# A slot order of an attention and mixture-of-experts kernel: pairs of score maxima behind the scores, VectorE's other work ahead of the maxima, top-2 steps spread over two slots, routing weights multiplied by GpSimd

## The reference, cut to what matters

```python
h = _layernorm(x) * (1 + ca) + sa
q, k, v = (split_heads(binlinear(h, W, b)) for W, b in ((Wq, bq), (Wk, bk), (Wv, bv)))
att = softmax(einsum('bhtd,bhsd->bhts', q, k) * scale)
x = x + ga * binlinear(merge(einsum('bhts,bhsd->bhtd', att, v)), Wp, bp)
h = _layernorm(x) * (1 + cb) + sb
shared = einsum('bsi,hi->bsh', silu(h @ shared_gate.T) * (h @ shared_up.T), shared_down)
probs = sigmoid(h @ router_w.T + routing_bias)
scores, indices = top_k(probs, 2)
scores = scores / sum(scores)                       # the two routing weights of a token
combined = sum over the two chosen experts of score * (silu(h @ gate_w[e]) * (h @ up_w[e])) @ down_w[e]
x = x + gb * (shared + combined)
```

## Time and profile before

| | |
|---|---|
| three runs | 663.35, 664.64, 675.9 us; median 664.64 us |
| profiled execution | 667.65 us, span 665.6 us |
| mean granted TensorE clock of its span | 0.969 of full speed |
| attention's paired slots | 78.03 to 464.14 us of the span |
| busy share of the span: TensorE, VectorE, ScalarE, GpSimd | 91%, 77%, 61%, 43% |

### The profile page before, as it was taken

The page is one execution under the profiler, slowest core; times in us unless marked ns, Lnnn a source line. Parts: engine busy times, 40 slices in busy tenths (PEclk is TensorE's granted clock), DMA queues, the critical chain, the costliest instruction groups (busy, mean ns, idle before and its releaser), DMA issues.

```text
span 665.6 us, 11786 instructions
## 1 busy us (share of the span) xinstructions
PE 602.6 (91%) x3693; PEld 270.0 (41%) x3693; DVE 511.2 (77%) x1068; ACT 409.0 (61%) x858; POOL 284.0 (43%) x333
## 2 busy tenths in 40 slices
PE   5979999998998999999899999989999899999935
PEld 2422222222222322222232222222256599999931
DVE  5559887988989898897888889898246876676627
ACT  2126777776776777767677677767944256666620
POOL 4205021352553355266155233313353447777740
PEclk9659999999999999999999999999999999999978
DMA  3523333332333344333332333311610222333328
GB/s 103 153 54 87 96 88 103 104 100 75 98 88 105 107 111 119 93 99 93 104 108 70 111 95 105 82 49 37 199 33 0 78 74 85 94 88 93 83 101 297
DMA packets 50205, 64.27 MB, mean 97 GB/s; under 512 B 11093, under 2 KB 34679, under 8 KB 50144
## 3 DMA queue, kind: packets, MB, share of 16 engines
q1 hardware_dynamic: 42788, 50.45, 27.4%
q0 software_dynamic: 4320, 8.47, 3.7%
q10 hardware_dynamic: 3036, 4.61, 2.1%
HBM read 45.70 MB, written 17.92 MB: 96 GB/s over the span
## 4 chain that ended last, share of the span: by engine, by line
PE 45%; DVE 20%; ACT 10%; issue 10%; DMA 6%; POOL 6%; SPq 1%; ACTq 1%; POOLq 0%; DVEq 0%
PE pv L1518 11%; DVE neg_max L1069 11%; PE st L1507 10%; ACT pt L861 6%; PE mx L1490 5%; POOL results L804 5%; PE mx L1655 3%; PE misc L1376 3%; PE misc L1403 2%; DMA routed<-rec,row_u 2%; PE mx L1486 2%; PE misc L1409 2%; PE st L1711 1%; PE misc L1433 1%; PE misc L1445 1%
## 5 line engine op out<-in xcount | busy, mean ns | idle before, releaser
L1069 DVE TENSOR_REDUCE neg_max<-mx 128x2 f32<-128x1024 f32 x256 | 307.1, 1217 | 58.3 <-PE mx L1493 43.0
L861 ACT ACTIVATE pt<-st 128x512 f32<-128x512 f32 x496 | 270.5, 599 | 113.2 <-PE st L1507 111.8
L1518 PE MATMUL pv<-pt,vs 128*32 128x512 f32 x1024 | 136.4, 605 | 0.3 <-ACT pt L861 0.3
L743 POOL DMA_INDIRECT routed<-rec,row_u x64 | 64.7, 1012 | 120.1 <-PE pv L1518 90.7
L804 POOL DMA_INDIRECT results<-qs,home_u x71 | 78.9, 1111 | 38.2 <-issue 21.9
L1507 PE MATMUL st<-even_qk 74*128 74x512 bf16 x256 | 83.7, 389 | 7.5 <-ACT pt L861 3.7
L1507 PE MATMUL st<-qs,ks 74*128 74x512 bf16 x240 | 76.5, 383 | 6.2 <-ACT pt L861 3.7
L1493 PE MATMUL mx<-upper 64*128 64x512 bf16 x224 | 73.5, 383 | 0.0
L413 POOL TENSOR_TENSOR qk_r<-qk_f,qk_parts 128x512 f32<-128x512 f32 x15 | 17.4, 1162 | 94.4 <-ACT qk_f L846 66.0
L985 ACT ACTIVATE vs<-st 128x256 f32<-128x256 f32 x71 | 27.3, 384 | 41.0 <-PE st L1711 41.0
L1507 PEld LDWEIGHTS st<-even_qk 74*128 74x128 bf16 x256 | 20.6, 99 | 75.5 <-ACT pt L861 53.8
(11 more groups left out here) (204 smaller groups left out, 867.3 us busy)
## 6 DMA issues: line engine op xcount, KB each, us to landing
ks<-routed SPq DMA_DIRECT2D x71, 65.0 KB, 1.9
even_qk<-q_parts SPq DMA_DIRECT2D x48, 96.0 KB
qs<-q_parts SPq DMA_DIRECT2D x48, 96.0 KB
ks<-k_parts SPq DMA_DIRECT2D x48, 96.0 KB
even_qk<-k_parts SPq DMA_DIRECT2D x36, 96.0 KB
q_parts<-qk_parts SPq DMA_DIRECT2D x21, 128.0 KB
k_parts<-qk_parts SPq DMA_DIRECT2D x21, 128.0 KB
upper<-q_parts SPq DMA_DIRECT2D x56, 48.0 KB
```

Of the source, the lines that this page charges most:

```text
L743: pool.indirect_dma_start(out=routed_dram, out_offset=bass.IndirectOffsetOnAxis(ap=row_u[:, k, t:t + 1], axis=0), in_=rec[b.par][:, k, t, ...
L861: act.activation(pt[n % 2][:, hh, :], score_bank(b, n, hh), ACT.Exp, scale=SCALE).then_inc(exp_done, 1)
L1069: dve.tensor_reduce(neg_max[g % 2][:, pair::PAIRS, t], mx_bank[f % 2][:], AX_X, ALU.max, negate=True).then_inc(mx_free, 1)
L1518: last = pe.matmul(pv_bank[32 * hh:32 * (hh + 1), :], vs[b.par][:, j, HG * g + hh, :], pt[n % 2][:, hh, :], start=(n % Y_SLOTS == 0), stop ...
```

## The change

Four things are moved; nothing is computed otherwise.

1. In slots with paired fills, TensorE makes both fills after the four scores and ahead of the products; before, they stood between the second and the third score, ahead of `between`.
2. In those slots VectorE does the slot's other work first and both maxima behind it; before, one maximum stood ahead and one behind.
3. `likeliest` (slot 13) ends with the sum and its reciprocal instead of the four `max_index`, which `choose` (slot 14) now begins with.
4. The two products of the routing weights are done by GpSimd (`choice_weights`), between the two `split_qk` of a batch; the indirect DMAs wait for them.

```diff
+            def choice_weights(b):
+                hold(pool, route_chain, CHOOSE_STEPS * b.n + SUM_STEPS)
+                pool.wait_ge(rows_free, b.n + 1)
+                for k in range(K_TOP):
+                    pool.tensor_tensor(rec[b.par][:, k, :, C], top_p[:, :, k], p_rsum[:], ALU.mult).then_inc(weights_ready, 1)
...
                 if b.const < B - 2:
                     split_qk(pool, b.plus(2), 0)
+                if not first:
+                    choice_weights(b.plus(-1))
+                if b.const < B - 2:
                     split_qk(pool, b.plus(2), 1)
...
                 for n in range(SLOTS):
                     fills = fills_at(b, n)
-                    maxima(fills[0])
+                    if not side_by_side(fills):
+                        maxima(fills[0])
...
+                    if side_by_side(fills):
+                        maxima(fills[0])
                     maxima(fills[1])
...
+                    together = side_by_side(fills)
                     scores(b, n, 0)
                     scores(b, n, 1)
-                    for f in fills[0]:
-                        max_scores(f)
-                    together = bool(fills[0]) and paired(fills[0][0])
-                    if together:
-                        max_scores(fills[1][0])
+                    if not together:
+                        for f in fills[0]:
+                            max_scores(f)
                     between(b, n, first, last)
                     scores(b, n, 2)
...
                     scores(b, n, 3)
-                    for f in fills[1][1:]:
+                    for f in fills[0] + fills[1] if together else fills[1][1:]:
                         max_scores(f)
```

More of the change, by code:

```diff
@@ L341, in adaln_block @@
         BATCH_ROWS = 16 * K_TOP * TT
-        CHOOSE_STEPS = 2 + 2 * TT + 3 + 1
+        SUM_STEPS, LIKELY_STEPS = 2 + TT + 2, 2 + TT + 2 + TT
+        CHOOSE_STEPS = LIKELY_STEPS + 2
         AHEAD, B0, B1, B_LAST = Batch(-1), Batch(0), Batch(1), Batch(B - 1)
@@ L376, in fills_at, with side_by_side @@
             return ([f], [f + 1]) if f < 2 * SLOTS * B else ([], [])
+        def side_by_side(fills):
+            return bool(fills[0]) and paired(fills[0][0])
         def m_slots(first):
@@ L755, in scatter_in_slots @@
                     if i == 0:
+                        hold(pool, weights_ready, K_TOP * (b.n + 1))
                         hold(pool, rows_ready, b.n + 1)
@@ L798, in _ @@
             modulate2(B_LAST)
+            choice_weights(B_LAST)
             scatter(B_LAST)
@@ L1117, in likeliest, with choose @@
                     link(dve.max(top_p[:, t, :], probs[:, t, :]), b, 3 + t, wait=t == TT - 1)
+                link(dve.tensor_tensor(p_sum[:], top_p[:, :, 0], top_p[:, :, 1], ALU.add), b, SUM_STEPS - 1)
+                link(dve.reciprocal(p_rsum[:], p_sum[:]), b, SUM_STEPS, wait=False)
+            def choose(b):
                 for t in range(TT):
[L1119 to L1129, removed]
+                    link(dve.max_index(top_e[:, t, :], top_p[:, t, :], probs[:, t, :]), b, SUM_STEPS + t + 1, wait=t == TT - 1)
+                link(dve.tensor_copy(top_ef[:], top_e[:, :, 0:K_TOP]), b, LIKELY_STEPS + 1)
                 link(dve.tensor_tensor(chosen[:], expert_no[:].unsqueeze(1).unsqueeze(1).to_broadcast([P, K_TOP, TT, E]),
```

## The result

The changed kernel takes 676.32 us in the median of 4 runs (675.36 to 681.92), the kernel before 667.21 in 4 runs on the same chip: a ratio of 1.0167, with a 95% interval of 1.0085 to 1.0248. Some executions run in a slower state (the 675.9 us among those before is one), so every ratio here compares only the executions outside it and is not the quotient of the medians beside it. By the ratio the changed kernel is slower by about 11 us. That is less than the 2.2% of the forecast; the time lies inside the forecast of 674 to 685 us; whether the loss is over or under 2% this measurement can't tell. A repeat on another chip gave 696.69 against 683.87, ratio 1.0161 [1.011, 1.0212].

A forecast was written before the change was run, and what follows sets the result against it. Empty slots were held bound by ScalarE's exponentials releasing the last two scores, slot 14 by VectorE. Batches 1 to 5 +7.4, batch 6 +3.4, batch 7 +2.4, batch 0 +1.2: +14.4, so 679.1 us, 2.2% slower; 8-in-10 range 668 to 689.

The forecast's parts named there:

- The likeliest case: Whole kernel: late pairs lengthen slots whose fourth score waits for exponentials; 679.1 us, 674 to 685, chance 0.68.
- The floor of an empty slot: Slots without other work: fourth score at 1.56, fills at 1.88 and 2.11, products at 2.42; 3.42 instead of 2.88.
- the faster rival: Paired slots: pairs take no time behind the scores, only waits for maxima go; 651.4 us, chance 0.06.
- Slots with a job of 1 us: Slots 4, 8, 14, with `project_out` or q/k projections in `between`: fourth score at 1.66, slot 3.50.
- Slot 15: Second fill, due at 2.13, goes at 2.41 after VectorE's maxima; with 0.13 for `ranks` the slot takes 3.85.
- The landing of the scatters: GpSimd's wait ahead of `modulate2` stays and shares slot 10's idle time; 0.2 us added in batches 2 and 4.
- Batch 0: From slot 8 on: 28.2 us against 26.99, counted as +1.2.
- The cheap change of tile: Fill to products costs 0.22 instead of 0.31, so 112 slots save 0.09 each; 669 us, chance 0.13.
- Pairs free behind the scores: Fills overlap or cost nothing, so the 0.54 isn't paid and 13.2 us of waits go; 651.4, chance 0.06.
- VectorE falls behind: Slots 3, 5, 13 to 15 lengthen by about 0.3 each, +1.5 a batch; 689 us, chance 0.10.
- The clock: TensorE's short idle pieces bring its clock down; one batch at the lower level costs 32 us: 711, chance 0.03.
- VectorE's cover and GpSimd's products: VectorE's late maxima remove nearly all 13.2 us of TensorE's waits, to about 2; the products on GpSimd cost nothing.

The follow-up runs named there:

- e9: Kernel before with the paired fills behind the fourth score, and GpSimd's second `split_qk` of a batch held until `choose` is over: 706.81 us, ratio 1.0328.
- e1: Changed kernel with its paired fills back between the second and third score: 695.59 us, ratio 1.0444 to the kernel before.
- e2: Kernel before with the paired fills behind the fourth score and nothing else changed: 719.94 us, ratio 1.0809.
- e5: Changed kernel with VectorE's old order, one maximum ahead of the slot's other work: 723.26 us, ratio 1.0462 to the kernel before.
- e7: Changed kernel with late fills and late maxima only in slots 8 and 14, old order elsewhere: 680.05 us, ratio 0.9837 to the kernel before.
- e8: As e7, with the second fill between third and fourth score in slots 3, 6, 7 and 15: 674.87 us, ratio 0.9756 to the kernel before.
- e10: Changed kernel with the two routing-weight products back on VectorE, in `choose`: 693.53 us, ratio 1.016 to the kernel before.

## Why the prediction was nearly right

The likeliest case came about, by its mechanism, and its size was too large. Step by step:

**The floor of an empty slot: right.** 3.42 forecast, 3.41 or 3.42 measured in slots 2, 3, 5, 6, 7, 10, 11 and 13. The one figure that no row of before showed, fill to products, is 0.31 (387.35 to 387.66), the end that I took. Products stand 0.86 behind the fourth score, as I had put the point that decides against the faster rival.

**Slots with a job of 1 us: 0.08 too long each.** For slots 4, 8 and 14 I put the third score at 1.44 and so the fourth at 1.66, by the 0.99 from a job behind fills to the score behind it. That price held a change of tile at its front: the job's second matmul stands 0.21 behind its first in slot 4 before (344.02 and 344.23), and 0.11 in the changed kernel (354.28 and 354.39). Behind a score slot 14's job comes after 0.45 and takes 0.86 (389.10 to 389.96), the third score is at 1.31, and the fourth is still released by ScalarE at 1.57. The slots are at the floor. The Trainium skill ("TensorEngine Tiling (Array Packing)", Key Properties) has the drain at a change of tiling mode; the row agrees that the step from score to this job, both without packed tiles, has none.

**Slot 15: 0.29 too long.** I had the maxima of slot 14 end 2.35 into slot 15. They ended at 393.93, 1.85 in, ahead of the second fill at 2.11. I had let the maxima start at 3.15 in slot 13 and added the rest; in the trace they start 2.85 into it (388.09 less 385.24), and `choose` costs less than I took. The slots of the forecast add up to 57.33, which I rounded up to 57.4. Slot 15's 0.29, 0.24 in slots 4, 8 and 14 together and 0.05 in slot 9, less 0.04 in slot 12, are the 0.5 between 57.33 and 56.82.

**The landing of the scatters: not there.** I added 0.2 to batches 2 and 4; batch 4 takes 56.81, like batch 5, and so has lost the 0.34 as well by which it was longer before (56.32 against 55.98). GpSimd's wait for the landing is 2.6 at the longest, where the kernel before has 4.8. Why is not shown: longer slots alone don't do it, since in e9, with slots as long, slot 10 still takes 3.74, 3.67 and 3.72 in batches 2 to 4.

**Batches 6 and 7: right within half a us.** +3.0 for +3.4, and +2.3 for +2.4.

**Batch 0: 0.5 too short.** Slot 13 took 4.03, since `misc` was held: TensorE's timeline there:

```profile
102.36 0.44 PE L1580 MATMUL misc<-ident,x 128*128 128x128 f32 x2 [1.10 <-DVE m_rows L1098]
```

`split_max` (line 1098) ended at 102.31 there; it stands behind maxima (99.45 to 101.81) that now start later, and it frees the bank. That is a cost of the late fills in a place where I had only looked at banks of `mx`. In later batches slot 13 has no job that needs `misc`.

**The sum.** The terms: batches 1 to 5 +3.8 for +7.4, batch 6 +3.0 for +3.4, batch 7 +2.3 for +2.4, batch 0 +1.7 for +1.2; together +10.8 for +14.4. The term that was mis-sized is the steady batch, 5 x 1.4 for 5 x 0.84, and there the slots with jobs and slot 15; the other 0.8 is the landing, 0.4 that I added and 0.4 by which batches 1 to 4 were longer than batch 5 before and are no longer.

**The rivals.** The cheap change of tile fell with 387.66. *Pairs free behind the scores* fell with it. *VectorE falls behind* didn't happen in the changed kernel, but it is what e1, e2 and e5 do (+3.5 to +8.7 a batch over before, the lower clock in e2 and e5 included): late fills and VectorE's new order hold only together. *The clock* stayed up in the changed kernel's paired slots, yet it fell in e2 and e5, and once or twice in e1, e7 and e8. The Trainium skill ("TensorE: Matmul & The Clock Gate", HAM oscillation) warns of idle gaps; I weighed it by slot 14's 1.26 alone and gave it 0.03, and that row turned out not to be a safe bound.

**VectorE's cover and GpSimd's products: right.** The waits of the paired fills for maxima are gone (I had left 2 us), and the products' place costs nothing (e10).

**One sign was put wrong.** I had written that ScalarE's wait for scores would grow by 0.5 a slot. In the empty slot 13 it went from 0.43 to 1.09, but over the whole span only from 111.8 to 121.6 us: slots with waits for VectorE, 14 above all, give back what the empty ones add (ScalarE is idle for 2.80 us of slot 14 before and for 0.64 after). It didn't fit my own sum either, in which a batch of 16 slots grows by 1.4.

## What to carry to other kernels

Ask of each instruction on the bounding engine what it hides behind: work that fills a wait for another engine is free, and moving it behind the wait puts all of it on the path, here 0.54 us in slots 0, 1, 5 and 13 of batch 5. Whether something else can take its place in the wait differs from slot to slot, so place it slot by slot; here late fills in two of 16 slots and half late ones in four turned +1.7% into -2.4%. And before undoing one part of a change to see its worth, ask which other part it needs: here late fills with the old order of VectorE cost 8.1% (3.3% when the clash with GpSimd is kept away, e9), the new order with early fills 4.4%, both together 1.7%.

## What the runs showed of the hardware that I had not expected

Some small operations of VectorE on SBUF last until GpSimd's operation beside them is over: 1.15 us in place of 0.16 for a sum of four elements (e2, e9), 1.03 in place of 0.19 for `marks`, 0.97 in place of 0.16 for a cast in e5, beside a GpSimd operation of 1.15. Not all do. In the kernel before, beside a GpSimd operation from 384.94 to 386.09, `next_row` (line 1141), with one input in PSUM, kept its 0.15, while `picked` (line 1143), with both inputs in SBUF, took 0.43 in place of the 0.23 of batches without that neighbour. Maxima read from PSUM keep their length: the second of the two from 391.58 in the changed kernel (2.35 together) runs beside a GpSimd operation of 1.15 that starts at 392.69. The Trainium skill ("GPSIMD Engine Reference", Specifications) says that GpSimd's SBUF interfaces are shared with VectorE and that instructions with two SBUF inputs or in a 2-port mode contend; the sum and `marks` fit that, and for the cast, with one input, no run here shows which mode it is in.

TensorE's clock went from 2.4 to 1.2 GHz behind waits of 1.84 us (e2) and 1.02 us (e5), and not behind one of 1.26 in slot 14 of six batches of the kernel before. The same wait can do either: 1.02 us in slot 15 of e5 left the clock up in batch 1 and was followed by its fall in batches 2 to 5. It also fell in slot 0 of batch 1 in e7 and e8 (0.69 and 0.68 over the slot, behind waits of 1.39 and 1.51 us for a DMA), and twice in e1, in slot 6 of batch 1 and slot 12 of batch 2, with no wait of TensorE there over 0.74 us; other batches have the same waits without a fall. In e2 each fall lengthened two slots by 3.1 and 2.6 us over those of e9, the wait itself included. Which idle time counts was not tried.
